# Moving two transposes, the input copy and the output store within the slots of a software-pipelined transformer layer, with a new table of PSUM banks

## The chip, the cores and the metric

The kernel runs on one core of one Trainium2 chip. The metric is the device time of one execution in microseconds (us), median of the runs of one kernel on the same chip.

## The reference, cut to what matters

The input x is 16 sequences of 256 tokens by 256 features in fp32. One layer is computed on each sequence, with no coupling between sequences:

```python
qkv = x @ Wqkv + bqkv                      # 16 query heads, 4 key/value heads, head size 16
q, k, v = jnp.split(qkv, [D, D + KV], axis=-1)
k, v = jnp.tile(...), jnp.tile(...)        # each key/value head serves 4 query heads
scores = jnp.einsum('bqhd,bkhd->bhqk', q, k) / HD
prob = jax.nn.softmax(scores, axis=-1)
out = jnp.einsum('bhqk,bkhd->bqhd', prob, v).reshape(b, s, D) @ Wout + bout
x = _layernorm(x + out)
gate, up = jnp.split(x @ ternary_quant(w_gate_up).T, 2, axis=-1)   # 2 x 1024 wide
h = jax.nn.silu(gate) * up
x = _layernorm(x + rms_norm(h) @ ternary_quant(w_proj).T)
```

## The kernel before, in words

**Slots.** Each engine has its own instruction stream, written by one `slot` function per engine and called for the slots t = 0, 1, 2, ... (`run_slots`). A sequence (called a batch in the code, b = 0 to 15) takes eight slots of the pipeline, and every stage has a fixed offset: the stage with offset o of batch b stands in slot t = 8b + o. So a stage recurs in all slots with the same t mod 8. Below, "slot m" (m = 0 to 7) means any slot with t mod 8 = m. Eight to ten stages of up to six batches are in flight at once. The slots up to t = 63 are unrolled, t = 64 to 127 are a hardware loop of four iterations of 16 slots (with addresses and wait values in registers), and the rest is unrolled again. Within a slot the order of the `if` blocks in the source is the order on the engine; engines wait for each other by semaphores only.

**The stages that matter here**, with their offset and the slot m in which they recur:

- LOAD_X (0, m = 0): SP (SyncE) issues the DMA of the sequence into `xn`, line 416. X_T (1, m = 1): TensorE (PE) transposes it, four 128x128 blocks, lines 635 to 638, after waiting for that DMA. X_HIGH (1): ScalarE (ACT) copies the result from PSUM to `xT`, lines 750 to 753. PROJ_Q and PROJ_K (2): projections from `xT`. So the DMA is issued one slot before it is used.
- SAVE_QK (2), STACK_QK (3) and STACK_REST (7): SP writes the projected q and k to DRAM and reads them back in another layout (`q_st`, `k_st`, lines 402 and 409). LOAD_RES (23, m = 7): SP loads the sequence again as residual, line 430.
- PROJ_V (7, m = 7): two transposes of `kv_f` on PE, lines 639 to 642, copied by VectorE (DVE) at line 918.
- MAX0 to MAX0 + 7 (from 9): in every slot two pairs of score matmuls (`max0` and `max1`, line 517), each into one PSUM bank, and for each a row maximum on DVE (line 807). SHIFT_T (13 and 17; m = 5 and 1): PE transposes the maxima.
- EXP0 (from 15): the scores again, line 526, then the exponential on ACT, line 717. PV0 (from 16): the product with v in every second slot, line 573.
- PROJ_O (27, m = 3): PE, line 470 from `wo` and `attT`; then O_ADD on DVE (line 932), the statistics (lines 935 and 939), and LN1_APPLY (28, m = 4) on DVE, line 923. X1_T (29, m = 5).
- FFN0 (from 31): gate and up matmuls, line 545, in every slot (in slot 5 behind `max0`, else at the slot's start); tanh on ACT (712), `gated` (855) and `h_f` (862) on DVE, `h_hi` on ACT (703), `h_lo` (976) and the sum of squares (981) on GpSimd (POOL). DOWN0 (from 33): line 558.
- LN2_APPLY (45, m = 5): POOL writes `y_out`, line 988, behind that slot's `h_lo` and sum of squares. STORE (47, m = 7): SP waits for it and issues the DMA to `out`, line 456; it is the last item of SP's slot, behind LOAD_RES and STACK_REST.

SP has one stream, too: while it waits in one item, nothing behind it is issued.

**The short banks.** Three PSUM banks (`short_ps`) are shared by `max0`, `max1`, the transposes and the projections. `BANK_TABLE` says which use of which slot m has which bank, and `SHORT_ORDER` gives the order of the uses within a slot. From both, `use_short` works out the previous user of the bank and makes PE wait until that one has been read (`released_by`: for `max` the row maximum, for `x` the copy to `xT`, for `o` the addition at line 932, and so on).

Of the kernel before, what the change touches and what calls it, by code (L numbers as in the profile page):

```python
# [24 lines left out]
P = 128  # L25
# [4 lines left out]
TT = S // P  # L30
DT = D // P
# [8 lines left out]
X_T = 1  # L40
# [6 lines left out]
PROJ_V = 7  # L47
# [16 lines left out]
MAX_FIRST = 5  # L64
LN2_STATS = 42
LN2_APPLY = 45
STORE = 47

X_HIGH = 1
Q_COPY = 2  # L70
# [16 lines left out]
INV = 40  # L87
RSTD2 = 43

SHORT_ORDER = ("max0", "shift0", "q", "pv0", "pv1", "max1", "x", "v", "x1", "o", "k", "att", "shift1", "sq")  # L90
SHORT_OFFSET = {"v": PROJ_V, "x": X_T, "q": PROJ_Q, "shift0": SHIFT_T[0], "shift1": SHIFT_T[1], "pv0": PV_T[0],
                "pv1": PV_T[1], "o": PROJ_O, "att": ATT_T, "k": PROJ_K, "x1": X1_T, "sq": SUM_SQ}
SHORT_USES = [(m, name) for m in range(SLOTS) for name in SHORT_ORDER
              if name not in SHORT_OFFSET or SHORT_OFFSET[name] % SLOTS == m]
BANK_TABLE = {0: {"max0": 2, "pv1": 0, "max1": 1, "sq": 2},
              1: {"max0": 1, "max1": 2, "x": 0, "shift1": 1},
              2: {"max0": 2, "q": 0, "max1": 2, "k": 1, "att": 0},
              3: {"max0": 2, "max1": 1, "o": 0},
              4: {"max0": 1, "max1": 2},
              5: {"max0": 2, "shift0": 0, "max1": 1, "x1": 2},  # L100
              6: {"max0": 0, "pv0": 1, "max1": 0},
              7: {"max0": 2, "max1": 1, "v": 0}}

BANK = {(m, name): BANK_TABLE[m][name] for m, name in SHORT_USES}

# [65 lines left out]
def wait(eng, sem, value):  # L171

    if isinstance(value, int):
        if value > 0:
            eng.wait_ge(sem, value)
    else:
        eng.wait_ge(sem, value)
# [34 lines left out]
def postln_layer(nc, x, Wqkv, bqkv, Wout, bout, w_gate_up, w_proj, out):  # L212
    ctx = ExitStack()
    with ctx:
# [250 lines left out]
        def _(pe):  # L465
# [35 lines left out]
            def use_short(n, name):  # L501

                if found := previous_use(n, SHORT_ORDER.index(name), short_users[BANK[n.t % SLOTS, name]]):
                    st, (_, _, released, per, extra) = found
                    wait(pe, released, st.count(per, extra))
                return short(n, name)
# [82 lines left out]
            def keep_clock(n, count):  # L589

                if n.it is not None or not CLOCK_FROM <= n.t < CLOCK_TO:
                    return
                turned = sum(at < n.t for at in W_TURN)
                if turned:
                    pe.wait_ge(w_ev, turned - 1)
                for _ in range(count):
                    pe.matmul(turn_banks[turned % 2][:, 0, 0:P], ident[:], ident[:], start=True, stop=True)  # L597

            def slot(n):
                if (st := n.chunk(FFN0)) and n.t % SLOTS != MAX_FIRST:  # L600
                    gate_up(n, st)
                if st := n.chunk(MAX0):
                    if st.it is None and st.b == 0 and st.s == 0:
                        pe.wait_ge(k_ones, 1)
                        pe.wait_ge(q_zeros[0], 1)
                        pe.wait_ge(q_zeros[1], 1)
                    max_scores(n, st, 0)
                if (st := n.chunk(FFN0)) and n.t % SLOTS == MAX_FIRST:
                    gate_up(n, st)
                if st := n.chunk(EXP0):  # L610
                    exp_scores(st)
                keep_clock(n, 2)
                if st := n.once(SHIFT_T[0]):
                    bank = use_short(n, "shift0")
                    turn_maxima(bank, st, 0)
                if st := n.once(PROJ_Q):
                    bank = use_short(n, "q")
                    wait(pe, xT_copied, st.count(1, 1))
                    if st.it is None and st.b == 0:
                        pe.wait_ge(wqkv_loaded, 16)  # L620
                    for m in range(DT):
                        last = products(bank[:, m * S:(m + 1) * S], [wqkv[:, k, m * P:(m + 1) * P] for k in range(DT)],
                                        [xT[:, k, :] for k in range(DT)])
                    last.then_inc(q_made, 1)
                for half in range(2):
                    if st := n.once(PV_T[half]):
                        bank = use_short(n, f"pv{half}")
                        wait(pe, pv_copied, st.count(2, half + 1))
                        turn(bank, [pv_sb[:, g, t * P:(t + 1) * P] for g in range(2) for t in range(TT)], pv_turned)
                if st := n.chunk(MAX0):  # L630
                    max_scores(n, st, 1)
                keep_clock(n, 2)
                if (st := n.chunk(PV0)) and st.s % 2:
                    times_v(st)
                if st := n.once(X_T):
                    bank = use_short(n, "x")
                    wait(pe, x_loaded[st.par], st.count2(16, 16))
                    turn(bank, [xn[:, st.par, t, k * P:(k + 1) * P] for k in range(DT) for t in range(TT)], xT_made)
                if st := n.once(PROJ_V):
                    bank = use_short(n, "v")  # L640
                    wait(pe, k_copied, st.count(1, 1))
                    turn(bank, [kv_f[:, t * P:(t + 1) * P] for t in range(TT)], v_made)
                if st := n.once(X1_T):
                    bank = use_short(n, "x1")
                    wait(pe, x1_done, st.count(TT, TT))
                    turn(bank, [x1[:, st.par, t, k * P:(k + 1) * P] for k in range(DT) for t in range(TT)], x1_turned)
                if st := n.once(PROJ_O):
                    bank = use_short(n, "o")
                    wait(pe, attT_copied, st.count(1, 1))
                    if st.it is None and st.b == 0:  # L650
                        pe.wait_ge(wo_loaded, 16 * (2 * G + 1))
                    for t in range(TT):
                        last = products(bank[:, t * D:(t + 1) * D], [attT[:, m, t * P:(t + 1) * P] for m in range(DT)],
                                        [wo[:, m, :] for m in range(DT)])
                    last.then_inc(o_made, 1)
                if st := n.once(PROJ_K):
                    bank = use_short(n, "k")
                    last = products(bank[:, 0:S], [wqkv[:, k, D:] for k in range(DT)],
                                    [xT[:, k, :] for k in range(DT)])
                    last.then_inc(k_made, 1)  # L660
                if st := n.once(ATT_T):
                    bank = use_short(n, "att")
                    wait(pe, att_done, st.count(4, 4))
                    turn(bank, [att[:, t, m * P:(m + 1) * P] for m in range(DT) for t in range(TT)], att_turned)
                if (c := turned_piece(n, 0)) is not None:
                    turn_weights(c)
                if st := n.chunk(DOWN0):
                    down(st)
                if st := n.once(SHIFT_T[1]):
                    bank = use_short(n, "shift1")  # L670
                    turn_maxima(bank, st, 1)
                if st := n.once(SUM_SQ):
                    bank = use_short(n, "sq")
                    wait(pe, h_summed, st.count(FT - 1, FT - 1))
                    for t in range(TT):
                        last = pe.matmul(bank[:, t:t + 1], sq_sum[:, st.par, t * P:(t + 1) * P], ones[:],  # L676
                                         start=True, stop=True)
                    last.then_inc(sq_summed, 1)
# [5 lines left out]
        def _(act):  # L684
# [23 lines left out]
            def slot(n):  # L708
                if st := n.chunk(FFN0):
                    wait(act, ffn_made, st.count(8, st.s + 1))  # L710
                    wait(act, gated_done, st.count(8, st.s - 1))
                    act.activation(tanh[:, st.s % 2, :], gate_up_bank(n, st, 0), ACT.Tanh, scale=0.5  # L712
                                   ).then_inc(tanh_done, 1)
                if st := n.chunk(EXP0):
                    wait(act, exp_scored, st.count(8, st.s + 1))
                    wait(act, pv_done, st.count(4, st.s // 2 - 1))
                    act.activation(probs[:, st.s % 4], exp_ps[:], ACT.Exp).then_inc(exp_done, 1)  # L717
# [21 lines left out]
                if st := n.chunk(H_HIGH0):  # L739
# [7 lines left out]
                        wait(act, h_summed, st.count(FT - 1, max(st.s - 2, 0)))  # L747
                        dst = h_sq[:, st.s % 2, :]
                    act.activation(dst, h_f[:, st.s % 2, :], ACT.Square).then_inc(h_squared, 1)  # L749
                if st := n.once(X_HIGH):  # L750
                    wait(act, xT_made, st.count(1, 1))
                    wait(act, k_made, st.count(1, 0))
                    high(xT[:], both(n, "x")).then_inc(xT_copied, 1)
                if st := n.once(X1_HIGH):
                    wait(act, x1_turned, st.count(1, 1))
                    wait(act, ffn_made, st.count(8, -8))
# [294 lines left out]
```

## Time and profile before

| | us |
|---|---|
| median of 3 runs | 607.46 |
| lowest, highest | 606.27, 610.3 |
| the profiled execution | 606.27 |
| its span, first to last instruction | 604.5 |
| mean granted TensorE clock | 0.981 of full speed |

One execution was recorded. All terms are read from that one, whose own time is 606.27 us: 604.5 us of span and 1.8 us around it. "Busy" counts an instruction from its start to its end; matmuls overlap, so the sum of neighbours is longer than the time that they take. "Idle before, released by" says how long an engine stood still ahead of an instruction and which instruction's end let it go on. L545 is line 545 of the kernel. Times of single instructions are microseconds from the span's start.

### The profile page before, as it was taken

To read this page: it belongs to the slowest core of one execution; us is meant where nothing else is said; L and a number is where in the kernel's file an instruction comes from. 1 tells how busy PE (TensorE), PEld (TensorE's weight loads), DVE (VectorE), ACT (ScalarE), POOL (GpSimd) and SP (SyncE) were. 2 spreads that over 40 slices of the span, in tenths; PEclk is the share of its full clock that TensorE was granted. 3 is DMA by queue.
4 is the path that set the end of the run, shared out by engine and by line. 5 is a ranking of instruction groups with operands and counts; after the bars stand their busy time and mean duration, and the time that the engine had idled before them with its cause. 6 is when DMAs were issued, how large, how long until landed. Compare 5 with 4: busy or idle time off the path is not lost.

```text
span 604.5 us, 14155 instructions
## 1 busy us (share of the span) xinstructions
PE 552.6 (91%) x4368; PEld 465.3 (77%) x4368; DVE 442.2 (73%) x1033; ACT 371.7 (61%) x738; POOL 330.7 (55%) x437
## 2 busy tenths in 40 slices
PE   5669999999999999999999999999999999898983
PEld 5657777778788787878787888878787877687973
DVE  7965755777877778776778777787867777865675
ACT  5454853666666666756566666667576666566652
POOL 5565851254555555563654555464646465466673
PEclk9797998999999999999999999999999999999998
DMA  7964355344351716153544526170625444010001
GB/s 236 156 133 53 86 84 97 73 97 72 81 105 58 130 39 110 41 113 77 98 88 85 99 64 121 44 119 22 133 51 105 80 96 90 2 37 18 3 18 36
DMA packets 53932, 49.08 MB, mean 81 GB/s; under 512 B 6144, under 2 KB 53888, under 8 KB 53888
## 3 DMA queue, kind: packets, MB, share of 16 engines
q1 hardware_dynamic: 51152, 47.60, 39.3%
q10 hardware_dynamic: 2736, 0.92, 0.7%
q8 instruction: 24, 0.39, 0.3%
q14 instruction: 20, 0.16, 0.1%
HBM read 33.29 MB, written 14.68 MB: 79 GB/s over the span
## 4 chain that ended last, share of the span: by engine, by line
PE 72%; DVE 16%; issue 4%; DMA 3%; POOL 2%; ACT 1%; ACTq 1%; SPq 1%; DVEq 0%; POOLq 0%
PE ffn_ps L545 16%; PE pv_ps L573 10%; PE short_ps L470 10%; PE short_ps L517 9%; PE exp_ps L526 8%; PE down_ps L558 7%; PE short_ps L581 7%; DVE row_max L807 4%; DVE st L935 2%; DVE r L932 2%; DVE gated L855 2%; DMA q_st<-shift_lo 1%; PE short_ps L676 1%; PE ffn_ps L597 1%; DMA wgu_raw<-in_L_ffn_w_gate_up_dram 1%
## 5 line engine op out<-in xcount | busy, mean ns | idle before, releaser
L807 DVE TENSOR_REDUCE row_max<-short_ps 128x2 f32<-128x512 f32 x256 | 173.8, 681 | 65.9 <-PE short_ps L517 65.7
L976 POOL TENSOR_TENSOR h_lo<-h_f,h_hi 128x256 fp32r<-128x256 f32 x128 | 94.7, 740 | 202.3 <-ACT h_hi L703 201.4
L717 ACT ACTIVATE probs<-exp_ps 128x1024 f32<-128x1024 f32 x128 | 131.0, 1024 | 41.5 <-PE exp_ps L526 39.5
L517 PE MATMUL short_ps<-k_st,q_st 65*128 65x256 f32 x512 | 116.8, 310 | 28.1 <-DVE row_max L807 23.4
L712 ACT ACTIVATE tanh<-ffn_ps 128x256 f32<-128x256 f32 x120 | 45.8, 382 | 121.7 <-PE ffn_ps L545 105.2
L517 PEld LDWEIGHTS short_ps<-k_st,q_st 65*128 65x128 f32 x512 | 83.1, 192 | 45.5 <-DVE row_max L807 17.0
L526 PE MATMUL exp_ps<-q_st,k_st 67*128 67x512 f32 x256 | 81.7, 400 | 1.4 <-DMA q_st<-shift_lo 1.3
L545 PE MATMUL ffn_ps<-x1T_hi,wguT 128*128 128x256 f32 x480 | 80.4, 290 | 2.6 <-DVE h_f L862 2.5
L981 POOL TENSOR_TENSOR sq_sum<-sq_sum,h_sq 128x256 f32<-128x256 f32 x105 | 78.0, 743 | 0.0
L558 PE MATMUL down_ps<-wpT,h_hi 128*128 128x256 f32 x256 | 75.2, 316 | 2.2 <-POOL h_lo L976 2.2
L545 PE MATMUL ffn_ps<-x1T_lo,wguT 128*128 128x256 f32 x480 | 77.2, 283 | 0.0
L573 PE MATMUL pv_ps<-probs,v_ones 128*32 128x256 f32 x1024 | 69.4, 389 | 0.0
L545 PEld LDWEIGHTS ffn_ps<-x1T_hi,wguT 128*128 128x128 f32 x480 | 65.2, 190 | 4.3 <-issue 3.6
L558 PE MATMUL down_ps<-wpT,h_lo 128*128 128x256 f32 x256 | 66.4, 282 | 0.0
L545 PEld LDWEIGHTS ffn_ps<-x1T_lo,wguT 128*128 128x128 f32 x480 | 65.0, 188 | 0.5
L855 DVE SCALAR_TENSOR_TENSOR gated<-tanh,ffn_ps 128x256 f32<-128x256 f32 x120 | 49.3, 411 | 14.8 <-ACT tanh L712 14.7
L862 DVE TENSOR_TENSOR h_f<-gated,ffn_ps 128x256 f32<-128x256 f32 x120 | 50.5, 421 | 6.1 <-DVE gated L855 2.2
L703 ACT ACTIVATE h_hi<-h_f 128x256 fp32r<-128x256 f32 x128 | 52.2, 408 | 1.5 <-DVE h_f L862 1.5
L558 PEld LDWEIGHTS down_ps<-wpT,h_hi 128*128 128x128 f32 x256 | 48.5, 189 | 5.9 <-POOL h_lo L976 3.6
L558 PEld LDWEIGHTS down_ps<-wpT,h_lo 128*128 128x128 f32 x256 | 48.6, 190 | 0.4
L470 PE MATMUL short_ps<-xT,wqkv 128*128 128x256 f32 x192 | 47.9, 386 | 0.0
L749 ACT ACTIVATE h_sq<-h_f 128x256 f32<-128x256 f32 x112 | 45.6, 407 | 0.0
(102 smaller groups left out, 888.7 us busy)
## 6 DMA issues: line engine op xcount, KB each, us to landing
q_st<-q_dram SPq DMA_DIRECT2D x128, 128.0 KB, 4.1
q_dram<-q_p SPq DMA_DIRECT2D x16, 512.0 KB, 3.0
xn<-in_L_attn_x_dram SPq DMA_DIRECT2D x16, 256.0 KB, 4.3
k_st<-k_dram SPq DMA_DIRECT2D x64, 64.0 KB, 2.3
res<-in_L_attn_x_dram SPq DMA_DIRECT2D x16, 256.0 KB, 4.5
out_dram<-y_out SPq DMA_DIRECT2D x16, 256.0 KB, 4.0
wgu_raw<-in_L_ffn_w_gate_up_dram SPq DMA_DIRECT2D x8, 256.0 KB, 6.2
k_dram<-k_p SPq DMA_DIRECT2D x16, 128.0 KB, 3.0
```

Of the source, the lines that this page charges most:

```text
L470: last = pe.matmul(dst, a, b, start=start and i == 0, stop=stop and i == len(pairs) - 1)
L517: last = pe.matmul(bank[:, t * S:(t + 1) * S], q_st[0:PAD, st.par, head, t * P:(t + 1) * P], k_st[0:PAD, st.par, st.s % 4, :], start=True, ...
L526: last = pe.matmul(exp_ps[:, t, :], k_st[:, st.par, st.s % 4, t * P:(t + 1) * P], q_st[:, st.par, first_head(st.s):first_head(st.s) + 5:4, ...
L545: last = pe.matmul(gate_up_bank(n, st, half), wguT[:, k, c:c + P], x1T[a][:, st.par, k, :], start=first and k == 0, stop=a == 1 and k == D ...
L558: last = pe.matmul(down_ps[:, t, :], h_p[a][:, st.s % 4, t * P:(t + 1) * P], wpT[:, st.s, :], start=(st.s == 0 and t == 0 and a == 0), sto ...
L573: last = pe.matmul(pv_ps[r:r + 32, s % 4 // 2, :], v_ones[:, st.par, t, s % 4, :], probs[:, s % 4, t, i, :], start=(t == 0), stop=(t == TT ...
L703: return act.activation(dst, src, ACT.Identity)
L717: act.activation(probs[:, st.s % 4], exp_ps[:], ACT.Exp).then_inc(exp_done, 1)
L807: dve.tensor_reduce(row_max[:, st.par, head * TT:(head + 1) * TT], short(n, f"max{i}")[:].rearrange("p (t k) -> p t k", t=TT), AX.X, ALU.m ...
L855: dve.scalar_tensor_tensor(gated[:, st.s % 2, :], tanh[:, st.s % 2, :], 1.0, gate_up_bank(n, st, 1), ALU.add, ALU.mult).then_inc(gated_don ...
L976: pool.tensor_tensor(h_p[1][:, st.s % 4, :], h_f[:, st.s % 2, :], h_p[0][:, st.s % 4, :].bitcast(F32), ALU.subtract).then_inc(h_lo, 1)
L981: pool.tensor_tensor(sq_sum[:, st.par, :], sq_sum[:, st.par, :], h_sq[:, st.s % 2, :], ALU.add).then_inc(h_summed, 1)
```

## The change

Three edits. (1) STORE goes from offset 47 to 45, so that SP waits for `y_out` and stores it in slot 5 instead of slot 7, ahead of the next slot 7's LOAD_RES and STACK_REST and the next slot 0's LOAD_X. (2) On PE the X_T and PROJ_V blocks go from behind `max1` and the product with v to just behind the exp scores of their slots (1 and 7), and X_HIGH on ACT goes from behind `h_hi` and the square to ahead of the exponential. (3) The bank table changes: in slot 2 the order of banks 2 and 0 is swapped (`max0`, `max1` in 0, `q`, `att` in 2), in slot 3 `max0` is in 0 and `o` in 2, in slot 4 `max1` is in 0.

```diff
-STORE = 47
+STORE = 45
-SHORT_ORDER = ("max0", "shift0", "q", "pv0", "pv1", "max1", "x", "v", "x1", "o", "k", "att", "shift1", "sq")
+SHORT_ORDER = ("max0", "x", "v", "shift0", "q", "pv0", "pv1", "max1", "x1", "o", "k", "att", "shift1", "sq")
 BANK_TABLE = {0: {"max0": 2, "pv1": 0, "max1": 1, "sq": 2},
-              1: {"max0": 1, "max1": 2, "x": 0, "shift1": 1},
-              2: {"max0": 2, "q": 0, "max1": 2, "k": 1, "att": 0},
-              3: {"max0": 2, "max1": 1, "o": 0},
-              4: {"max0": 1, "max1": 2},
+              1: {"max0": 1, "x": 0, "max1": 2, "shift1": 1},
+              2: {"max0": 0, "q": 2, "max1": 0, "k": 1, "att": 2},
+              3: {"max0": 0, "max1": 1, "o": 2},
+              4: {"max0": 1, "max1": 0},
               5: {"max0": 2, "shift0": 0, "max1": 1, "x1": 2},
               6: {"max0": 0, "pv0": 1, "max1": 0},
-              7: {"max0": 2, "max1": 1, "v": 0}}
+              7: {"max0": 2, "v": 0, "max1": 1}}
@@ PE, slot
                 if st := n.chunk(EXP0):
                     exp_scores(st)
                 keep_clock(n, 2)
+                if st := n.once(X_T):
+                    bank = use_short(n, "x")
+                    wait(pe, x_loaded[st.par], st.count2(16, 16))
+                    turn(bank, [xn[:, st.par, t, k * P:(k + 1) * P] for k in range(DT) for t in range(TT)], xT_made)
+                if st := n.once(PROJ_V):
+                    bank = use_short(n, "v")
+                    wait(pe, k_copied, st.count(1, 1))
+                    turn(bank, [kv_f[:, t * P:(t + 1) * P] for t in range(TT)], v_made)
                 if st := n.once(SHIFT_T[0]):
...
                 if (st := n.chunk(PV0)) and st.s % 2:
                     times_v(st)
-                if st := n.once(X_T):
-                    bank = use_short(n, "x")
-                    wait(pe, x_loaded[st.par], st.count2(16, 16))
-                    turn(bank, [xn[:, st.par, t, k * P:(k + 1) * P] for k in range(DT) for t in range(TT)], xT_made)
-                if st := n.once(PROJ_V):
-                    bank = use_short(n, "v")
-                    wait(pe, k_copied, st.count(1, 1))
-                    turn(bank, [kv_f[:, t * P:(t + 1) * P] for t in range(TT)], v_made)
@@ ACT, slot
                     act.activation(tanh[:, st.s % 2, :], gate_up_bank(n, st, 0), ACT.Tanh, scale=0.5
                                    ).then_inc(tanh_done, 1)
+                if st := n.once(X_HIGH):
+                    wait(act, xT_made, st.count(1, 1))
+                    wait(act, k_made, st.count(1, 0))
+                    high(xT[:], both(n, "x")).then_inc(xT_copied, 1)
                 if st := n.chunk(EXP0):
...
                     act.activation(dst, h_f[:, st.s % 2, :], ACT.Square).then_inc(h_squared, 1)
-                if st := n.once(X_HIGH):
-                    wait(act, xT_made, st.count(1, 1))
-                    wait(act, k_made, st.count(1, 0))
-                    high(xT[:], both(n, "x")).then_inc(xT_copied, 1)
```

## Rows read from the trace of the kernel before

**Rows 1.** The page: busy time of each engine, and the chain that ended last.
```profile
PE 552.6 (91%) x4368; PEld 465.3 (77%) x4368; DVE 442.2 (73%) x1033; ACT 371.7 (61%) x738; POOL 330.7 (55%) x437
...
PE 72%; DVE 16%; issue 4%; DMA 3%; POOL 2%; ACT 1%; ACTq 1%; SPq 1%; DVEq 0%; POOLq 0%
```

**Rows 2.** Waits of PE, by pair: us in total, times, longest us.
```profile
PE short_ps L517 <- DVE row_max L807: 23.4, 22, 2.4
```

**Rows 3.** Timeline of PE: start, us, operation, [idle before <- releaser].
```profile
99.03 0.48 PE L517 MATMUL short_ps<-k_st,q_st 65*128 65x256 f32 x2 [1.38 <-DVE row_max L807]
...
329.33 0.51 PE L517 MATMUL short_ps<-k_st,q_st 65*128 65x256 f32 x2 [1.10 <-DVE row_max L807]
329.67 0.64 PE L545 MATMUL ffn_ps<-x1T_hi,wguT 128*128 128x256 f32 x4
...
362.17 0.50 PE L517 MATMUL short_ps<-k_st,q_st 65*128 65x256 f32 x2 [1.10 <-DVE row_max L807]
...
525.63 0.47 PE L517 MATMUL short_ps<-k_st,q_st 65*128 65x256 f32 x2 [1.19 <-DVE row_max L807]
```

**Rows 4.** The chain of waits from 310 to 345 us: start, us, what.
```profile
312.26 0.47 PE exp_ps L526 x2
...
323.47 1.94 PE short_ps L470 x8
...
325.43 0.70 DVE r L932
```

**Rows 5.** Timeline of DVE in slots 4, 5 and 6.
```profile
328.25 0.42 DVE L862 TENSOR_TENSOR h_f<-gated,ffn_ps 128x256 f32<-128x256 f32 x1
328.59 0.68 DVE L807 TENSOR_REDUCE row_max<-short_ps 128x2 f32<-128x512 f32 x1
...
330.80 0.68 DVE L807 TENSOR_REDUCE row_max<-short_ps 128x2 f32<-128x512 f32 x1
...
334.88 0.69 DVE L807 TENSOR_REDUCE row_max<-short_ps 128x2 f32<-128x512 f32 x1 [1.52 <-PE short_ps L517]
```

**Rows 6.** Timeline of POOL: y_out in slot 5 of two batches.
```profile
334.11 2.43 POOL L988 TENSOR_SCALAR y_out<-r,mv,rstd 128x256 f32<-128x256 f32 x2
...
530.37 2.43 POOL L988 TENSOR_SCALAR y_out<-r,mv,rstd 128x256 f32<-128x256 f32 x2
```

**Rows 7.** Timeline of SP: DMA issues around slots 7 and 0.
```profile
139.16 1.84 SPq L402 DMA_DIRECT2D q_st<-q_dram  x4
141.05 0.43 SPq L416 DMA_DIRECT2D xn<-in_L_attn_x_dram  x1
...
329.71 0.40 SPq L430 DMA_DIRECT2D res<-in_L_attn_x_dram  x1
335.42 1.72 SPq L409 DMA_DIRECT2D k_st<-k_dram  x4
337.18 1.86 SPq L402 DMA_DIRECT2D q_st<-q_dram  x4
339.41 0.41 SPq L456 DMA_DIRECT2D out_dram<-y_out  x1
340.06 0.40 SPq L416 DMA_DIRECT2D xn<-in_L_attn_x_dram  x1
...
532.82 0.39 SPq L456 DMA_DIRECT2D out_dram<-y_out  x1
```

**Rows 8.** DMA issues at 141.0 us (KB, us to landing); then all loads of xn.
```profile
xn<-in_L_attn_x_dram SPq DMA_DIRECT2D x1, 256.0 KB, 4.8
...
DMA to landing us min/median/max: 3.3/4.3/6.4
```

**Rows 9.** Busy time by stretch (PE, PEld, DVE, ACT, POOL, PEclk, DMA), and a PE row.
```profile
100.80:104.20 3.40, 3.40 (x25) 1.91 (x25) 0.92 (x3) 0.23 (x1) 0.00 (x0) 0.52 0.35 57
572.00:576.00 4.00, 2.52 (x22) 2.31 (x20) 3.41 (x11) 2.10 (x6) 2.81 (x6) 1.00 0.01 4
...
576.29 0.63 PE L581 MATMUL short_ps<-ident,x 128*128 128x128 f32 x4 [1.76 <-DVE x L923]
```

## The prediction

> **What bounds the kernel now.** I read the page first: PE is busy for 552.6 of 604.5 us, and of the chain that ended last it holds 72%, DVE 16% [rows 1]. So PE sets the pace, and what stands in its way is worth looking for. The list of waits has one large entry for PE: 23.4 us in 22 waits of the score matmuls for the row maximum [rows 2]. The timeline of PE shows where: in the steady part one wait per batch, 1.10 us, always ahead of `max0` of slot 5, at 329.33 and again at 362.17, that is a period of 32.84 us per batch [rows 3]. From 99.03 (1.38 us) to 525.63 (1.19 us) it comes 14 times, once per batch [rows 3]. The bank table gives the cause: `max0` of slot 5 is in bank 2, last used by `max1` of slot 4, and DVE comes to that maximum late (328.59, 0.68 us [rows 5]) because slot 3's layer norm is on DVE from 325.43 [rows 4].
>
> **The bank table.** In the new table the previous user of that bank is `o` of slot 3, read by the DVE addition from 325.43 for 0.70 us [rows 4], long before. The wait goes. What is late next: the gate matmuls behind `max0` need `h_f` of slot 4, which ends at 328.25 + 0.42 = 328.67 [rows 5]; with 0.05 for the semaphore they start at 328.72 instead of 329.67 [rows 3], a gain of 0.95 us, not 1.10. The transpose of the maxima waits for the same late maximum, but has gate and exp matmuls ahead of it. The X1 transposes need the bank that `max0` of slot 5 leaves, 330.80 + 0.68 = 331.48 [rows 5], which is about when PE now comes to them. DVE itself gets nothing earlier there, it works without a break. Bounds: 0 (DVE takes it all back) and 1.10; I take 0.95, the value that the rows give.
>
> **X_T, PROJ_V and X_HIGH.** No instruction is added. On ACT the exponential of slot 1 now stands behind the copy of x and so starts some 1.0 us later; its readers, the exp scores of slot 2 and the product with v of slot 3, come over 1 us later still, so it costs nothing while x is on time. If x is late, PE, too, is late by as much, and the slack is kept. Banks cost nothing here either: `q` of slot 2 is now behind `max1` of slot 1, read long before. What the move does do is to ask for x earlier. X_T used to stand behind `max1` and the product with v. It now stands where the exp scores end, 312.26 + 0.47 = 312.73 [rows 4], one period on 345.57. With the 0.95 us won in slot 5, PE is there at 344.6.
>
> **The store.** SP is one stream. `y_out` ends at 334.11 + 2.43 = 336.54 [rows 6], and since DVE's work in slots 3 to 5 begins when `o` ends (325.41, 323.47 + 1.94 [rows 4]), `y_out` is 11.13 us behind `o` whatever PE wins in slot 5. So far SP had begun to stack keys at 335.42 and came to the store at 339.41, when it was long ready; then x was issued at 340.06 [rows 7]. Now SP stands in the store until 336.54, and behind it come the residual (until now issued at 329.71, out of the way), the keys, the queries and x. In the loop: wait over, and register work as between the other issues, 0.3; store 0.41; gap 0.37 (as from 337.18 + 1.86 to 339.41); residual 0.40; gap 0.15; keys 1.72; gap 0.04 [rows 7]. That is 3.4 us: the queries are issued from 339.95 instead of 337.18, x from 342.2 instead of 340.06 (0.3 behind the queries' 1.86). The residual is read by POOL in slot 1 and the keys by `max0` there, ahead of which both still land; I put nothing on them. In the unrolled part the register work is missing (530.37 + 2.43 to 532.82 is 0.02 us [rows 6, 7]), and the sum is 2.75 us.
>
> When does x land? The nearest rows are those of 139.16 and 141.05, a sequence of keys, queries and x with no store between: x landed 4.8 us after its issue, 6.7 us after the first query issue [rows 7, 8]. The queue drains at its own rate, so I count from the queries: 339.95 + 6.7 = 346.65. From below the bound is the shortest landing, 3.3 us [rows 8], 345.5; from above, with the store and the residual still in the queue, 6.4 us [rows 8], 348.6. I take 346.65, from the row with the same sequence.
>
> The Trainium skill, in "DMA: Bandwidth & Descriptors", section on the anatomy of one DMA, fits a time of 2.0 us plus bytes over 436 GB/s for the GpSimd path: 2.6 us for these 256 KB, by which x would be there at an estimated 344.8. The trace disagrees on this path: 4.3 us is the median [rows 8].
>
> **The cycle that follows.** From x to the end of `o` PE has the same work as now, 325.41 - 312.73 = 12.68 us [rows 4]. The ring is closed: `o` to `y_out` 11.13, SP 3.4, queries to landed x 6.7, semaphore 0.05, x to `o` 12.68: 33.96 us against 32.84, +1.1 us per batch in the loop. Unrolled it is 33.3, +0.45. PE arrives at 344.6 and waits 2.1 us for x in slot 1. That replaces the wait of 1.10 us.
>
> **Sum.** The first store is in slot 45. Before it the slot 5 of two batches (t = 29, 37) gains 0.95 each: -1.9. The loads of x behind a store are those of t = 48 to 120, ten: three unrolled or at the loop's entry, 3 x 0.45 = 1.4, and seven in the loop, 7 x 1.1 = 7.7. After the last load two slots 5 (t = 125, 133) gain again: -1.9. Net +5.3 us. Nothing else on the way out depends on the store's earlier slot.
>
> **The clock.** The granted clock was at 1.2 GHz (0.52) from 100.8 to 104.2 us, after PE had been idle for 1.38 us at 99.03 amid small matmuls, and stayed at 2.4 GHz (1.00) in 572 to 576, ahead of and during an idle time of 1.76 us amid dense ones [rows 3, 9]. The new wait is longer than both. A fall as long as that one (3.4 us) does 1.7 us of work, a loss of up to 1.7. Bounds: none, or ten times 1.7; the dense row is the nearest, so I take 1.5 falls, 2.5 us. By the Trainium skill ("TensorE: Matmul & The Clock Gate", on oscillation) waits for a DMA in each tile re-throttle the array each time; that is the third rival. Total: 606.3 + 5.3 + 2.5 = 614.1, so 614 us. The median of the runs lies 1.2 us above the profiled execution; that is inside what I can tell. Within 1% (601.4 to 613.5) counts as no change, about what a measurement of this kernel can tell.
>
> **Rivals.**
>
> *The load is on time, and the kernel is faster.* For it: the residual and the store leave before the queries, so the queue is emptier when x is issued; 3.3 us has been seen [rows 8]. Against: it was seen for loads issued late behind the queries. At 345.5 the ring is 32.8 us, the ten loads cost nothing, and the time is 606.3 - 3.8 = 602.5. If x were there at 344.6 or before, all 14 waits are won: 606.3 - 14 x 0.95 = 593. It decides at x landed by 345.5. (The skill's 2.6 us would give nearly this; the same page, on queues and rings, says that descriptors are taken in ring order, which speaks for a load that waits behind the queries.) Chance 0.25, half of it for under 601.4.
>
> *DVE takes the slot 5 gain back.* PE waits at `h_f` or at the X1 bank for what it won; the four free gains are lost, the ring stays: 606.3 + 9.1 + 2.5 = 618. For it: DVE has no gap from 325.43 to 333. Against: it is idle for 1.52 us in slot 6 [rows 5], so it is not the bound over a batch. Chance 0.1.
>
> *The clock falls in most batches.* Ten waits of 2 us, ten falls of 1.2 to 1.7 us: 611.6 + 12 to 17, about 626. For it: the wait is longer than the 1.38 us after which it fell. Against: the 1.76 us. Chance 0.15.
>
> *Forecast:* the ring through store and load, 0.5, with a range of its own of 607 to 620.
>
> **From this the numbers.** The faster side is half of the first rival and a little of the forecast's low end: 0.17. Same: the other half and the forecast below 613.5, 0.35. Slower: the rest, 0.48. The range leaves out the fastest and the slowest end: 598 to 626.
>
> **What would show it.** Right: no wait for the row maximum at `max0` of slot 5; instead a wait of 1.5 to 2.3 us of the transposes of `xn` for their DMA, about ten times, from t = 49 to 121; SP waits for `y_out`, with the store 3 us earlier, the residual behind it, x issued some 5.7 us behind the end of `y_out`; a period near 34 us in the loop; the exponential of slot 1 about 1 us behind its scores plus the wait. Wrong: no DMA wait at `xn` and a period under 32 us (then the landing was over-estimated), or a wait of PE for `h_f` of over 0.5 us in slot 5 (then the bank term was), or clock rows of 0.5 in the loop (then the third rival).

## The result, and the profile after

The changed kernel takes 613.94 us (median of 5 runs, 613.76 to 618.09) against 608.95 for the kernel before on the same chip (606.27 to 610.3): a ratio of 1.0111, 95% interval 1.0067 to 1.0155. It is slower by about 1%. The profiled execution took 615.71 us with a span of 613.9; the one of before stood at 606.27 and 604.5. So 9.4 us are to be found between the two traces.

The page of the changed kernel, the same two lines as in [rows 1] (busy time; the chain that ended last):
```profile
PE 561.6 (91%) x4368; PEld 470.4 (77%) x4368; DVE 443.1 (72%) x1033; ACT 370.3 (60%) x738; POOL 330.8 (54%) x437
...
PE 49%; DVE 12%; DMA 12%; SPq 9%; POOL 8%; issue 7%; ACT 1%; ACTq 1%; POOLq 0%; DVEq 0%
```
PE has the same 4368 matmuls and is busy for 9 us more: nothing was added to them, and the mean granted clock is lower, 0.966 against 0.981. The chain changed its character. Before, it was PE and DVE; now 29% of it is DMA, SP and POOL, though no transfer and no instruction was added. The pieces shown further down close to a ring through a load.

Waits of PE between 175 and 500 us of the changed kernel (us in total, times, longest):
```profile
PE short_ps L581 <- DMA xn<-in_L_attn_x_dram: 13.4, 10, 1.8
PE ffn_ps L545 <- DVE h_f L862: 2.5, 9, 0.4
```
In the same stretch of the kernel before, the only entry of this size was the wait for the row maximum, 11.2 us in ten. It is gone from this list, and ten waits of the `xn` transposes stand in its place. The early, unrolled part has its own: in the whole run the row maximum still has 6.8 us in 7 waits.

Timeline of PE, six of the ten waits (start, us, operation, idle before and its releaser):
```profile
179.08 1.00 PE L581 MATMUL short_ps<-ident,xn 128*128 128x128 f32 x4 [1.28 <-DMA xn<-in_L_attn_x_dram]
...
281.07 0.63 PE L581 MATMUL short_ps<-ident,xn 128*128 128x128 f32 x4 [1.09 <-DMA xn<-in_L_attn_x_dram]
...
297.31 0.74 PE L545 MATMUL ffn_ps<-x1T_hi,wguT 128*128 128x256 f32 x4 [0.26 <-DVE h_f L862]
...
314.52 0.66 PE L581 MATMUL short_ps<-ident,xn 128*128 128x128 f32 x4 [1.14 <-DMA xn<-in_L_attn_x_dram]
...
348.54 0.63 PE L581 MATMUL short_ps<-ident,xn 128*128 128x128 f32 x4 [1.79 <-DMA xn<-in_L_attn_x_dram]
...
416.90 0.63 PE L581 MATMUL short_ps<-ident,xn 128*128 128x128 f32 x4 [1.55 <-DMA xn<-in_L_attn_x_dram]
...
452.08 1.00 PE L581 MATMUL short_ps<-ident,xn 128*128 128x128 f32 x4 [1.44 <-DMA xn<-in_L_attn_x_dram]
```
From 281.07 to 314.52 is one period: 33.45 us, against 32.84 in [rows 3]. The line at 297.31 is slot 5, where before PE stood for 1.10 us at `max0`; now it stands for 0.26 at the gate matmuls.

SP of the changed kernel, the stretch that answers to [rows 7]:
```profile
304.53 0.41 SPq L456 DMA_DIRECT2D out_dram<-y_out  x1
305.22 0.40 SPq L430 DMA_DIRECT2D res<-in_L_attn_x_dram  x1
305.81 1.75 SPq L409 DMA_DIRECT2D k_st<-k_dram  x4
307.60 1.85 SPq L402 DMA_DIRECT2D q_st<-q_dram  x4
310.26 0.40 SPq L416 DMA_DIRECT2D xn<-in_L_attn_x_dram  x1
```
And its chain of waits between the two waits for x, the pieces that close the ring:
```profile
281.07 0.63 PE short_ps L581 x4
...
292.05 1.94 PE short_ps L470 x8
294.01 0.70 DVE r L932
...
299.95 0.42 ACT h_hi L703
...
300.43 0.29 POOL h_lo L976
...
301.85 2.44 POOL y_out L988 x2
...
307.60 0.43 SPq L402
...
310.26 4.21 DMA xn<-in_L_attn_x_dram
```
Read it as a circle: x lets PE come to `o`, `o` lets DVE and POOL make `y_out`, `y_out` lets SP past the store, SP issues the next x, and x lets PE go on. `o` ends at 293.99, `y_out` 10.3 us later at 304.28; the queries follow 3.3 us after that at 307.60, and x is there 6.9 us behind them, at 314.47. From x to `o` it is 12.9 us.

The clock, in stretches right behind four of the ten waits, and over nine periods (PE, PEld, DVE, ACT, POOL, PEclk, DMA share, GB/s):
```profile
180.00:182.00 2.00, 2.00 (x19) 0.81 (x17) 0.69 (x1) 1.88 (x4) 0.00 (x0) 0.50 0.01 4
350.00:353.00 3.00, 3.00 (x18) 2.21 (x11) 0.68 (x3) 1.32 (x3) 1.91 (x3) 0.50 0.00 0
419.00:421.00 2.00, 2.00 (x12) 1.75 (x9) 0.30 (x2) 0.69 (x3) 1.55 (x3) 0.50 0.00 0
453.00:455.00 2.00, 2.00 (x19) 0.81 (x17) 0.69 (x1) 1.80 (x4) 0.00 (x0) 0.50 0.00 0
182.00:500.00 318.00, 303.33 (x2384) 252.40 (x2381) 233.34 (x557) 199.45 (x403) 171.47 (x233) 0.98 0.39 80
```
A PEclk of 0.50 is 1.2 GHz. PE is busy throughout these rows, and slow. The ten waits bound nine periods: 35.10, 33.59, 33.30, 33.45, 34.02, 34.57, 33.79, 35.18 and 35.46 us. The four that begin with a fall (the first, sixth, eighth and ninth) have a mean of 35.08, the other five 33.63. So by this comparison a fall costs 1.45 us. It lies between x and `o`, on the ring, where nothing takes it up.

The nine periods together are 308.5 us; the same nine batches of the kernel before took 296.4 (32.93 on average; most of them 32.84). That is 12.1 us lost in the middle, 6.3 by the ring (9 x 33.63 = 302.7) and 5.8 by the clock, and 2.7 won at both ends.

### The profile page after: what moved, and what is told of

Read it like the earlier page. It is cut to its first block, busy times and chain, and to the rows that moved or that the text cites. A ratio compares the mean times of both kernels' runs of the same rounds, so it can differ in the third digit from the quotient of the medians.

```text
span 613.9 us, 14163 instructions
## 1 busy us (share of the span) xinstructions
PE 561.6 (91%) x4368; PEld 470.4 (77%) x4368; DVE 443.1 (72%) x1033; ACT 370.3 (60%) x738; POOL 330.8 (54%) x437
## 4 chain that ended last, share of the span: by engine, by line
PE 49%; DVE 12%; DMA 12%; SPq 9%; POOL 8%; issue 7%; ACT 1%; ACTq 1%; POOLq 0%; DVEq 0%
PE short_ps L470 11%; PE ffn_ps L545 10%; DMA xn<-in_L_attn_x_dram 9%; PE pv_ps L573 7%; PE short_ps L517 5%; PE down_ps L558 5%; PE exp_ps L526 5%; PE short_ps L581 4%; SPq L402 4%; POOL y_out L988 4%; SPq L409 3%; DVE st L935 2%; DVE r L932 2%; DVE gated L855 1%; DVE row_max L807 1%
## 5 line engine op out<-in xcount | busy, mean ns | idle before, releaser
L545 PE MATMUL ffn_ps<-x1T_hi,wguT 128*128 128x256 f32 x480 | 82.5, 295 | 6.6 <-DVE h_f L862 6.5
L558 PE MATMUL down_ps<-wpT,h_hi 128*128 128x256 f32 x256 | 76.6, 321 | 2.2 <-POOL h_lo L976 2.0
L573 PE MATMUL pv_ps<-probs,v_ones 128*32 128x256 f32 x1024 | 71.8, 400 | 0.0
```

Of the source, the lines that this page charges most:

```text
L545: last = pe.matmul(gate_up_bank(n, st, half), wguT[:, k, c:c + P], x1T[a][:, st.par, k, :], start=first and k == 0, stop=a == 1 and k == D ...
L558: last = pe.matmul(down_ps[:, t, :], h_p[a][:, st.s % 4, t * P:(t + 1) * P], wpT[:, st.s, :], start=(st.s == 0 and t == 0 and a == 0), sto ...
L573: last = pe.matmul(pv_ps[r:r + 32, s % 4 // 2, :], v_ones[:, st.par, t, s % 4, :], probs[:, s % 4, t, i, :], start=(t == 0), stop=(t == TT ...
```

## The experiments

My theory after the result: two harmless shifts close a ring. The store's wait delays the issue of x, the bank table and the early place of X_T let PE ask for it sooner, and neither alone would cost. (A batch's trip round such a circle of waits is the ring; a fall is a stretch at 1.2 GHz.) The rivals were that one part costs by itself (the early store through its queue, or the moved transposes through banks and ACT), and that the falls of the clock are most of the loss.

### The store back, everything else kept

```
 STORE = 45    ->    STORE = 47
```


> The changed kernel with the store put back to offset 47; the bank table and the early X_T, PROJ_V and X_HIGH stay. Theory (the early store holds SP until y_out is done, x is issued late, and PE waits for it): the ten waits of the xn transposes for their DMA are gone, slot 5 has no wait for the row maximum, the period is 32.84 - 0.95 = 31.9 us, and the time is about 606.3 - 14 x 0.95 = 593 us, 3.4% under the changed kernel. Rival (x is asked for too early by PE itself, wherever the store stands): DMA waits at xn stay at about 1 us per batch, and the time is 603 us or more. Rival (DVE takes the gain of slot 5 back): no DMA waits, but 606 us.

Measured: 594.47 us (593.93 to 595.5), ratio 0.9776, interval 0.9732 to 0.982. Waits of PE from 175 to 500 us:
```profile
PE ffn_ps L545 <- DVE h_f L862: 2.8, 10, 0.4
```
And the clock over the stretch of the last row above:
```profile
182.00:500.00 318.00, 315.15 (x2550) 265.48 (x2548) 249.01 (x599) 211.65 (x428) 182.79 (x249) 1.00 0.44 88
```
No wait for `xn` is left, no fall either, and in the same 318 us PE gets through 2550 matmuls instead of 2384. The period is 32.03 us. One number decides between 2.2% faster and 1.1% slower than the kernel before. A second set of six runs of this same kernel gave the same:

> Again the changed kernel with the store at 47, beside the next one, to tell whether the early X_T and PROJ_V are worth anything once the store is out of the way. Theory: the product with v in slots 1 and 7 and the weight load behind it have a little less to wait for, 0.2 us per loop batch (32.02 against 32.23 us), some 3 us in all: 593 to 596 us. Rival: the 0.8% seen between the two came from the start phase or the chip's state, and both are within 0.3%.

Measured: 596.06 us (593.28 to 597.2), ratio 0.98, interval 0.9768 to 0.9832.

### The store alone

```
 # kernel before
 STORE = 47    ->    STORE = 45
```


> The kernel before with only the store at offset 45. Theory: the ring is 'o' to y_out 11.1, SP 3.4, queries to landed x 6.9 (as measured in the changed kernel), 0.05, and from the old place of X_T to the end of 'o' 11.45 us, in sum 32.9 us against a period of 32.84 of PE itself. So almost nothing: x lands just when PE comes to it, waits of 0 to 0.3 us, 606 to 609 us. Rival (the early store costs by itself, by DMA traffic or by SP's other issues): 612 us or more.

Measured: 609.89 us (606.53 to 612.51), ratio 1.0001, interval 0.997 to 1.0033. Waits of PE, 175 to 500 us:
```profile
PE short_ps L517 <- DVE row_max L807: 11.2, 10, 1.2
PE short_ps L581 <- DMA xn<-in_L_attn_x_dram: 3.2, 7, 0.9
```
The old waits stay and small ones for `xn` come up behind them. So x is late even with the transposes at their old place, by more than the 0 to 0.3 us that I had expected, and no loop period shows a lower clock. In this recorded execution (612.51 us, the longest of its ten) the nine periods have a mean of 33.30 us, against 32.93 before. If it costs anything, it is less than 0.33%, the upper end of the interval. By itself the early store is cheap.

### The bank table alone

```
 # kernel before
-  2: {"max0": 2, "q": 0, "max1": 2, "k": 1, "att": 0},
-  3: {"max0": 2, "max1": 1, "o": 0},
-  4: {"max0": 1, "max1": 2},
+  2: {"max0": 0, "q": 2, "max1": 0, "k": 1, "att": 2},
+  3: {"max0": 0, "max1": 1, "o": 2},
+  4: {"max0": 1, "max1": 0},
```


> The kernel before with only the new bank table of slots 2, 3 and 4. Theory: max0 of slot 5 no longer waits for the row maximum, gate waits about 0.1 to 0.3 us for h_f instead, 0.95 us less in each of 14 batches: 593 us, ratio 0.978. Rival (DVE is the bound behind it and takes it back): 604 to 607 us.

Measured: 599.18 us (596.62 to 600.73), ratio 0.986, interval 0.981 to 0.991. Waits of PE, 175 to 500 us:
```profile
PE ffn_ps L545 <- DVE h_f L862: 3.4, 11, 0.6
```
The wait for the row maximum is gone and a short one for `h_f` is what is left, as in slot 5 of the changed kernel. Over nine periods it has 289.9 us, or 32.2 each. I had expected 593 us, about the time of the first experiment, and missed it by 6, so I ran both again, side by side:

> Again the kernel before with the new bank table alone. Theory: 3 us slower than with the early moves, 596 to 600 us. Rival: within 0.3% of it.

Measured: 597.66 us (595.53 to 600.68), ratio 0.9832, interval 0.98 to 0.9865, where the kernel with the early transposes had 0.98. The intervals overlap. In the trace of the first of these two sets eight of the nine periods have a mean of 32.03, that of the first experiment; the ninth is 33.64 and makes the whole difference in that stretch. Both traces have one such long period, at the same place: ACT's issue of one small load (`shift_lo`) takes 1.68 and 1.54 us there instead of 0.61, ACT comes late to its copy of q, and PE waits 0.66 and 0.52 us for it. The kernel before has it too (1.46 us); in the two traces with the early transposes and the store at 47 the issue at that place took 0.61. Why isn't shown. Whether the early transposes are worth anything by themselves these runs don't settle; in the other periods they show nothing.

### The early transposes alone

```
 # changed kernel
 STORE = 45    ->    STORE = 47
 BANK_TABLE, slots 2 to 4: as before
```


> The kernel before with only the moves of X_T, PROJ_V and X_HIGH (store at 47, old bank table). Theory: x has landed 1.1 us before PE comes to it at its new place, so no DMA wait in the loop and no gain but some 0.1 us per batch at slot 7's max1: 604 to 607 us. Rival (the early copy on ACT delays the exponential and with it PE, or the load is late): 609 us or more.

Measured: 607.47 us (606.35 to 611.74), ratio 1.0001, interval 0.9973 to 1.0028. From 175 to 500 us:
```profile
PE short_ps L517 <- DVE row_max L807: 11.2, 10, 1.2
PE short_ps L581 <- DMA xn<-in_L_attn_x_dram: 0.2, 1, 0.2
```
The two moved blocks and the copy moved on ACT cost nothing and bring nothing. They do bring PE to the edge: 0.2 us of one wait shows that x comes just in time here.

### Store and bank table, transposes at the old place

```
 # kernel before
 STORE = 47    ->    STORE = 45
 BANK_TABLE, slots 2 to 4: as changed
```


> The kernel before with the store at 45 and the new bank table, but X_T, PROJ_V and X_HIGH at their old places. Theory: the ring through store and load rules. In the changed kernel a loop batch without a clock fall took 33.3 to 34.0 us; with x at its old place PE has 1.2 us less to do from x to 'o', so 32.1 to 32.8 us against 32.84 before; waits of PE for x of 0.3 to 1.3 us, few or no clock falls; 599 to 605 us. Rival (what costs is the store's place alone): as much behind the banks-only kernel (599 us) as the changed kernel is behind the one with its store put back, 19 us, so 618 us. Rival (the early x asks for the load too early and that alone made the wait): no waits, 594 to 600 us.

Measured: 601.0 us (596.48 to 602.59), ratio 0.9871, interval 0.9817 to 0.9926. From 175 to 500 us:
```profile
PE ffn_ps L545 <- DVE h_f L862: 2.8, 10, 0.4
PE short_ps L581 <- DMA xn<-in_L_attn_x_dram: 1.4, 3, 0.8
```
With this seven of the eight combinations of the three parts have been run. Ratios to the kernel before: store 1.000, transposes 1.000, bank table 0.986 and 0.983, bank table and store 0.987, bank table and transposes 0.978 and 0.980, all three 1.011. No part by itself is slower than the kernel before, and both pairs that were run are faster. What turns is the price of the store: with the new bank table it costs 0.1 to 0.4% with x at its old place (0.987 against 0.986 and 0.983, intervals of half a percent to either side), and some 19 us, over 3%, with x at its early place (613.9 against 594.5). So it is the store and the early transposes that don't go together.

Store and transposes with the old bank table is the one pair that I didn't run. An estimate from the pieces: `y_out` came 11.13 us behind `o` with the old table, and with 3.32 to the queries, 6.87 to landed x, 0.05 and 12.92 from x to `o` the ring would be 34.3 us against 32.84, longer than with the new table. If so, that pair loses as well, and the new bank table isn't needed for the loss. No run shows it.

### The store behind the next load of x

```
 # changed kernel
 STORE = 45    ->    STORE = 48
```


> The changed kernel with the store at offset 48, where it stands behind LOAD_X on SP. Theory: x is issued some 0.8 us sooner than with the store at 47, and both are early enough, so the same as with 47: no DMA waits in the loop, 592 to 596 us. Rival (the store's traffic next to the load matters as well): under 592 us, or over 597 us.

Measured: 594.53 us (593.69 to 596.9), ratio 0.9745, interval 0.9691 to 0.9798. No wait for `xn` in the steady part, as at 47. Both places are equally good, and both beat the two kernels. So these two runs show no cost of the store's place as long as SP doesn't wait for `y_out` ahead of the loads.

### The load of x past SP

```
 # changed kernel, SP's slot
-  if (st := n.once(LOAD_X)) ...:
-      sp_wait(xT_made, st.count(1, -1))
-      sp.dma_start(xn[:, st.par], ...).then_inc(x_loaded[st.par], 16)
 # head of ACT's slot
+  if (st := n.once(LOAD_X)) ...:
+      wait(act, xT_copied, st.count(1, -1))
+      act.dma_start(xn[:, st.par], ...).then_inc(x_loaded[st.par], 16)
```


> The changed kernel (store at 45) with the load of x issued by ACT at the start of slot 0 instead of by SP. It takes x out of SP's stream, and leaves the bytes and the DMA engines as they are. Theory (SP's stream holds x back): x is issued about 1.2 us sooner and need not stand behind the queries in one queue; waits of PE for x fall from 1.1-1.8 to under 0.5 us, no clock falls, 595 to 602 us. Rival (the DMA engines' backlog of store, residual, keys and queries sets the landing): x lands as late as before, waits of 1 us or more, 608 us or more.

Measured: 600.65 us (600.06 to 604.15), ratio 0.9867, interval 0.9805 to 0.9929. Timeline of the two issuing queues around one load:
```profile
301.35 1.85 SPq L402 DMA_DIRECT2D q_st<-q_dram  x4
302.21 0.42 ACTq L707 DMA_DIRECT2D xn<-in_L_attn_x_dram  x1
```
Waits of PE for it, 175 to 500 us, and the longest of them with the clock behind it:
```profile
PE short_ps L577 <- DMA xn<-in_L_attn_x_dram: 4.4, 6, 1.5
...
308.50 0.66 PE L577 MATMUL short_ps<-ident,xn 128*128 128x128 f32 x4 [1.50 <-DMA xn<-in_L_attn_x_dram]
...
310.00:312.00 2.00, 2.00 (x18) 1.13 (x10) 0.12 (x1) 1.31 (x3) 0.84 (x2) 0.50 0.00 0
```
The store still holds SP, and the queries still leave late, but x no longer stands behind them in program order. It is issued 0.9 us behind the first of them instead of 2.7 (307.60 to 310.26 above), and takes longer to land: over the ten loads behind a store a median of 5.4 us instead of 4.6. The period falls from 33.63 to 32.8 and the waits from ten to six. The time came out as expected, the details only in part: three of the six waits are over 0.5 us (1.50, 0.97 and 0.89), and the clock fell once, behind the longest. So the late issue of x is a large part of the cost, and about half of what the earlier issue wins is given back in a longer landing. x also went through another engine's queue here, which wasn't told apart.

### The residual out of the way

```
 # changed kernel
 LOAD_RES = 23    ->    LOAD_RES = 21
```


> The changed kernel (store at 45) with the residual's load at offset 21 instead of 23, so that it stands ahead of the store on SP. It takes one issue of 0.69 us (0.40 and its gaps) and 256 KB out of the ring and leaves the rest. Theory (the ring's length is a sum of its terms): 0.7 us less wait per batch, ten times, and fewer clock falls, so 7 to 12 us less than the changed kernel: 602 to 607 us. Rival (the wait is set by something else): 612 to 615 us.

Measured: 602.25 us (599.0 to 607.16), ratio 0.9886, interval 0.9806 to 0.9966. From 175 to 500 us:
```profile
PE ffn_ps L545 <- DVE h_f L862: 3.6, 11, 0.8
PE short_ps L581 <- DMA xn<-in_L_attn_x_dram: 3.0, 6, 1.2
```
In the changed kernel the residual (slot 7) stood behind the store and cost SP 305.81 - 305.22 = 0.59 us of the ring. In slot 5, ahead of the store, it costs nothing there. The period is 32.67 us, 0.96 less than 33.63, and no fall of the clock is left in the steady part. From the issue of the store to that of x SP now takes 5.03 and 4.51 us in turn, where it took 5.73 and 5.40: 0.7 to 0.9 of the 0.96. The rest may be the emptier queue, which wasn't told apart. So one issue of 0.4 us ahead of the loads, and what it set off, was worth 11.7 of 613.9 us.

### The wait kept, PE busy in it

The waits could be told from the falls that follow them only by keeping PE at work while it waits. Nothing of the computation changes, the bank is written again by the transposes.
```
 # changed kernel, X_T
     bank = use_short(n, "x")
+    if n.it is not None or n.t >= 48:
+        for _ in range(8):
+            pe.matmul(bank[:, 0:P], ident[:], ident[:], start=True, stop=True)
     wait(pe, x_loaded[st.par], st.count2(16, 16))
```


> The changed kernel with eight 128x128 matmuls of the identity put ahead of the wait for x, into the bank that x will overwrite, in each batch from t = 49 on. They take about 1 us in which PE would stand idle, and change no load, store or bank. In the changed kernel the granted clock fell after four of the ten waits for x, and those three loop batches took 35.1 us on average against 33.6 us of the others. Theory (the falls are a cost of the idle time itself, about 1.4 us each): waits of 0 to 0.9 us, no falls in slots 0 to 2 of the loop, the loads land as late as before, 606 to 611 us. Rival (the extra time of those batches is the load's, and the low clock only goes with it): batches of 35 us stay, 612 to 616 us. Rival (the dummies delay x where it is on time): over 616 us.

Measured: 613.32 us (611.85 to 614.99), ratio 1.0093, interval 1.0063 to 1.0122. That is above the 606 to 611 of my theory and in the range of the first rival (612 to 616), but the batches of 35 us that the rival asked for aren't there. Timeline of PE, one place:
```profile
245.43 1.95 PE L617 MATMUL short_ps<-ident 128*128 128x128 f32 x16
```
The eight matmuls stand as sixteen and take 1.8 us up to the start of the next (247.21), more than most of the waits they were to fill. The clock stayed up (1.00 over the nine periods), but the filler itself had become the delay: the period is 33.96. I repeated it with five:

> As e9, with five identity matmuls instead of eight. In e9 each of the eight stood in the trace as two matmuls; the sixteen took 1.8 us and so covered the whole wait and more, the clock did not fall, and the time was that of the changed kernel. Five take 1.1 us, less than the 1.3 us that PE waits on average in the changed kernel. Theory (a fall costs some 1.4 us and idle time brings it): a rest of 0 to 0.7 us of waiting, no falls in the loop, 33.6 us per loop batch, 3 to 6 us less than the changed kernel: 608 to 611 us. Rival (the load alone sets the period and the falls are hidden in it): 613 to 615 us, 34.2 us per loop batch without falls.

Measured: 611.22 us (606.85 to 614.73, 12 runs), ratio 1.003, interval 0.9999 to 1.0062. The place again, and the clock over the nine periods:
```profile
281.86 1.28 PE L617 MATMUL short_ps<-ident 128*128 128x128 f32 x10
283.61 0.66 PE L581 MATMUL short_ps<-ident,xn 128*128 128x128 f32 x4 [0.47 <-DMA xn<-in_L_attn_x_dram]
```
```profile
182.00:500.00 318.00, 312.36 (x2513) 264.20 (x2513) 236.02 (x563) 201.15 (x406) 172.45 (x234) 1.00 0.41 82
```
Here the wait is filled, and in seven of the ten places 0.2 to 0.7 us of it are left, so there x is still the later of the two. In the other three no wait is left. The nine periods take 303.1 us, 33.68 each: close to the ring of the changed kernel without its falls (33.63), measured in another way. Against 308.5 the four falls cost 5.4 us, 1.34 each. The timed median lies 0.2 us above the range I gave, though its ratio is clearly under 1.0111. Filling the wait wins back the clock's share and no more; moving the store wins both. All of these are sums from one recorded execution of each kernel.

## Why the prediction was right

The mechanism, its place and its count were right: the wait for the row maximum went, the store, SP and the load of x closed a ring, and PE waited ten times for x. That 614.0 was forecast and the median is 613.94 is luck in the last digits. The forecast was a base of 606.3 and a change of +7.8 us. The base was the lowest of the five runs of the kernel before (median 608.95), and the change was +5.0 between the medians, +6.8 by the ratio, and +9.4 between the two recorded executions, from which all terms are read. Against those 9.4 the ring was taken too large and the clock too small, and what was then still missing was made up by the low base.

Of the prediction's own signs, those for being right came, some in weaker form: waits of 0.84 to 1.79 us, three of the ten within the 1.5 to 2.3 given, ten from t = 49 to 121, and x issued 6.0 us behind the end of `y_out` instead of 5.7. One sign for being wrong came too: clock rows of 0.5 in the loop, named as the mark of the third rival.

**The bank table: right in kind, a little too large.** 0.95 us per batch was the value taken, 13.3 us in 14 batches. The wait for the row maximum went, and what came next was `h_f`, as worked out (0.26 us at 297.31). Alone it shortens the period from 32.84 to 32.03 us, 0.81, and in 14 batches that would be 11.3 us; the two timings say 8.5 and 10.2 (0.014 and 0.0168 of about 608), and one long period in each trace takes part of it back.

**The moved transposes and the copy: right.** No cost found in the experiment that has them alone. That they ask for x earlier is what makes the ring long enough to hold PE. The exponential of slot 1 did move behind the copy of x (315.78, its scores done at 313.2), and nothing waited for it.

**The store: right in its order, a little off in two pieces.** SP waits for `y_out`, then issues store, residual, keys, queries and x, with 3.32 us to the queries (3.4 forecast) and x issued 5.98 us behind `y_out` (5.7). Queries to landed x took 6.87 us (6.7), x to `o` 12.92 (12.68). The step that failed is "`y_out` is 11.13 us behind `o` whatever PE wins in slot 5": it took 10.29. I had let it follow from DVE alone. The chain shows its true predecessor: POOL has `h_lo` and the sum of squares ahead of `y_out`, they need ACT's `h_hi`, and that stands behind the tanh and the exponential of slot 5, which wait for PE's matmuls. ACT before and after (start, us, operation):
```profile
331.29 1.02 ACT L717 ACTIVATE probs<-exp_ps 128x1024 f32<-128x1024 f32 x1
332.21 0.41 ACT L703 ACTIVATE h_hi<-h_f 128x256 fp32r<-128x256 f32 x1
...
299.03 1.02 ACT L721 ACTIVATE probs<-exp_ps 128x1024 f32<-128x1024 f32 x1
299.95 0.41 ACT L703 ACTIVATE h_hi<-h_f 128x256 fp32r<-128x256 f32 x1
```
`h_hi` ran 6.80 us behind `o` before and 5.96 now. So `y_out` got 0.84 us of what PE had won. In sum the loop's ring is 33.63 us instead of 33.96, and the wait of PE for x is 13.4 / 10 = 1.34 us instead of 2.1. The other part of that difference is that PE arrived later than forecast, 32.3 us after the x before (281.07 to 313.38) and not 31.9.

**The clock: right in kind, too small.** I took 1.5 falls, 2.5 us; in the traces it is four falls, 5.4 us by the filled waits and 5.8 by the periods. The step was to take the dense row of 1.76 us as the nearest to every new wait. One such row couldn't carry a count of ten. The Trainium skill ("TensorE: Matmul & The Clock Gate", on oscillation) says of another kernel that its DMA wait in each tile throttles the array again each time. The trace agrees for four of the ten waits and not for the other six.

**The sum.** For the ring over nine periods my terms give 2 x 0.45 + 7 x 1.1 = 8.6 us; it was 6.3. For the clock 2.5; it was 5.8. Together 11.1 against 12.1 in the middle. The ends, two gained slots 5 on either side less 0.45 for the entry to the ring, were -3.4 and came to -2.7, which makes 7.7 forecast against 9.4. What is missing there I didn't trace piece by piece; the start has an exchange of its own: the fall at 100.8 us of the kernel before [rows 9] is gone (1.00 from 101.0 to 104.4), and a new one stands at 83 to 87 (0.58), behind a wait of 0.64 us for x, which the early transposes ask for sooner there too.

**The rivals.** *The load is on time*: refuted here, since x landed 6.9 us behind the queries and PE was there 1.1 us sooner. It wasn't far off: x landed 20.5 us behind `o`, and the rival asked for 20.1 (345.5 - 325.41). The better of its two times was good: with x on time the kernel takes 594.5 (593 forecast for all 14 waits won). The Trainium skill ("DMA: Bandwidth & Descriptors", anatomy of one DMA) fits its time for loads issued by GpSimd, an estimate of 2.6 us for this size. These loads, issued by SP, took longer: the median of the changed kernel's 16 loads of x is 4.7. *DVE takes the gain back*: no, `h_f` holds PE for 2.5 us in nine waits and the bank gain is there when the store is out of the way. *The clock falls in most batches*: part of it came, four of ten; a fall cost what it had said (1.4 us, in its 1.2 to 1.7), but its 626 counted ten of them.

## What to carry to other kernels

SP issued its transfers in order here, so the wait put ahead of its next loads became part of those loads' latency. Put a store behind the loads whose data is wanted soonest (594.5 us here), or move what is ready ahead of the wait (602.3), or issue the load from another engine (600.7). Ask of each part of a change not only what it costs alone but whether it closes a ring with another; here the early store cost 0.1 to 0.4%, within the noise, with x asked for at the old time, and some 19 us with x asked for 1.2 us sooner. And when a wait is short against the period, price the lower clock behind it as a second term, since here four falls cost almost as much as the ring itself.

## What was unexpected of the hardware

- The clock fell from 2.4 to 1.2 GHz after waits of 1.28, 1.79, 1.55 and 1.44 us amid dense matmuls, and not after others of 1.32, 1.29, 1.09, 1.14, 0.84 and 1.65 us in the same code. With x issued by ACT it fell after 1.50 us and not after 0.97 and 0.89. The length of the wait alone doesn't tell which. With the wait filled by matmuls there was no fall in nine periods, in either of the two kernels that did it.
- One fp32 matmul of the 128x128 identity with itself stands as two in the trace: eight gave sixteen rows and 1.95 us, five gave ten and 1.28 us.
- When x landed followed the queries more than its own issue. In the kernel before, from 100 us on, all twelve loads of x landed 6.3 to 7.3 us behind the first of the four query loads: in 4.4 and 4.8 us where x was issued 1.9 us behind it, in 3.3 to 3.5 us where it was 3.4. Through ACT's queue nine loads, issued 0.5 to 1.0 us behind the first query load, landed 5.3 to 7.1 us behind it.
